# Byte addresses worked out together ahead of the matmuls of a mixture-of-experts tile loop

## The reference, cut to what matters

```python
def _L0_ffn_ref(x, W1, W2, Wr):          # E, DFF, TOPK = 8, 512, 2
    probs = softmax(einsum('btd,ed->bte', x, Wr))
    topk_vals, topk_idx = top_k(probs, 2)
    gate = topk_vals / topk_vals.sum(-1) at topk_idx, 0 elsewhere
    h = silu(einsum('btd,efd->btef', x, W1))
    y = einsum('btef,edf->bted', h, W2)
    return einsum('bte,bted->btd', gate, y)
x = layernorm(x + _L0_ffn_ref(x, W1, W2, Wr))
```

## Time and profile before

| | |
|---|---|
| median of three runs | 1368.81 us |
| profiled execution | 1367.97 us |
| its span, first to last instruction | 1366.2 us |
| TensorE matmul busy | 1071.8 us, 78% |
| VectorE busy | 857.5 us, 63% |
| ScalarE busy | 700.8 us, 51% |
| GpSimd busy | 478.8 us, 35% |
| mean granted TensorE clock | 0.90 of full speed |

### The profile page before, as it was taken

One profiled execution on the slowest core, in us unless ns is written; L12 is line 12 of the kernel. 1 busy time (PEld: TensorE's weight loads), 2 busy tenths in 40 slices (PEclk: granted clock), 3 DMA queues, 4 the chain that ended last, 5 costly groups with the idle time before them and its releaser, 6 DMA issues.

```text
span 1366.2 us, 33527 instructions
## 1 busy us (share of the span) xinstructions
PE 1071.8 (78%) x11050; PEld 875.2 (64%) x11051; DVE 857.5 (63%) x2570; ACT 700.8 (51%) x1284; POOL 478.8 (35%) x588
## 2 busy tenths in 40 slices
PE   3888888884999999999997510079999999999992
PEld 2777777873888888888876300066666666666672
DVE  3788888884788888888886660034445444444451
ACT  3666666663776776767763400044444444444441
POOL 3233333332010010010002427716555655565555
PEclk9999988896999999999997555589999999999996
DMA  6900000000000000000000001121111111111100
GB/s 184 186 17 15 15 15 15 15 9 18 13 11 21 10 10 19 10 18 11 0 1 1 1 16 53 53 57 34 42 37 44 32 36 40 40 35 36 41 17 1
DMA packets 91572, 42.03 MB, mean 31 GB/s; under 512 B 46146, under 2 KB 87372, under 8 KB 91524
## 3 DMA queue, kind: packets, MB, share of 16 engines
q1 hardware_dynamic: 86532, 32.83, 11.2%
q0 software_dynamic: 4992, 8.54, 2.0%
HBM read 20.57 MB, written 16.57 MB: 27 GB/s over the span
## 4 chain that ended last, share of the span: by engine, by line
PE 50%; DVE 20%; issue 12%; ACT 12%; POOL 4%; DMA 0%; DVEq 0%; POOLq 0%; ACTq 0%; SPq 0%
PE bank L439 15%; PE bank L440 12%; PE bank L441 10%; PE bank L541 5%; POOL xd L395 3%; DVE at L912 3%; ACT XTa L745 3%; PE bank L527 3%; ACT qz L745 3%; DVE X L989 3%; DVE mx L896 3%; PE bank L518 2%; DVE st L979 2%; ACT vz_self L754 1%; DVE XTa L888 1%
## 5 line engine op out<-in xcount | busy, mean ns | idle before, releaser
L823 ACT ACTIVATE pr<-bank 128x512 f32<-128x512 f32 x92 | 55.0, 597 | 264.4 <-PE bank L441 262.6
L439 PE MATMUL bank<-XTa,qz 128*128 128x128 f16 x768 | 145.2, 225 | 37.8 <-ACT XTa L745 37.8
L912 DVE TENSOR_TENSOR at<-bank,rc 64x32 f32<-64x32 f32 (+1 forms) x768 | 153.5, 200 | 14.4
L439 PE MATMUL bank<-cth,W 128*128 128x128 f16 x384 | 88.3, 230 | 86.5 <-DMA cth<-xd 85.5
L759 ACT ACTIVATE pr<-bank 128x512 f32<-128x512 f32 x192 | 114.1, 594 | 78.7 <-PE bank L518 77.5
L331 POOL TENSOR_SCALAR ve<-mv 128x4 f32<-128x4 f32 x55 | 12.9, 235 | 396.2 <-DVE mv L983 240.9
L896 DVE TENSOR_REDUCE mx<-bank 128x8 bf16<-128x512 f32 x192 | 132.9, 692 | 26.3 <-PE bank L441 20.7
L441 PE MATMUL bank<-XTa,qz 128*128 128x128 f16 x768 | 145.8, 226 | 0.0
L440 PE MATMUL bank<-XTa,qz 128*128 128x128 f16 x768 | 145.7, 226 | 0.0
L763 ACT ACTIVATE pt<-bank 128x512 f32<-128x512 f32 x192 | 113.2, 590 | 59.5 <-PE bank L527 59.1
L1079 DVE TENSOR_TENSOR ql<-pr,qh 128x512 f16<-128x512 f32 x46 | 49.1, 1068 | 145.5 <-ACT qh L824 143.2
(11 more groups left out here) (209 smaller groups left out, 3516.1 us busy)
## 6 DMA issues: line engine op xcount, KB each, us to landing
xd<-blank SPq DMA_DIRECT2D x1, 6072.0 KB, 35.0
X<-xd SPq DMA_DIRECT2D x23, 264.0 KB, 2.9
X<-x_dram SPq DMA_DIRECT2D x16, 256.0 KB, 2.8
wst<-w_dram SPq DMA_DIRECT2D x16, 256.0 KB, 2.7
cin<-ctx_in_dram SPq DMA_DIRECT2D x16, 256.0 KB, 2.9
out_dram<-X,dest POOLq DMA_INDIRECT x92, 2.3
mraw<-mask_dram SPq DMA_DIRECT2D x32, 32.0 KB, 2.7
xd<-XTa,pos POOLq DMA_INDIRECT x64, 2.3
```

Source lines behind the costliest of these rows:

```text
L439: nc.tensor.matmul(out_, lh, rh, start=start, stop=False, **kw)
L823: nc.scalar.activation(s32[n % 4][:], bank[n % 4][:], ACT.Silu, scale=IWS)
L912: m = nc.vector.tensor_tensor(dst, src, r, ALU.mult)
```

## The change

`up` and `down` call it ahead of their loop over f; in `down` it stands after the two waits. The matmuls, their operands and their order are the same, and so are all other engines' programs.

```diff
@@ -645,6 +645,7 @@
+            W8 = W12[:].bitcast(U8)
             H, Y = bank[0:4], bank[4:8]
             pairs = pe.alloc_register("pairs")
@@ -655,13 +656,19 @@
             def offsets(word, k):
-                return [pe.snap(word // E ** (2 * k + 1 - e) % E * (2 * DFF)) for e in range(2)]
+                return [pe.snap(word // E ** (2 * k + 1 - e) % E * (4 * DFF)) for e in range(2)]
+
+            def weights(at, stationary):
+                v = [W8[:, bass.ds(at + 2 * P * n, 2 * P)].bitcast(F16) for n in range(2 * FC)]
+                for ap in v:
+                    pe.lower_ap(ap, for_matmul_weights=stationary)
+                return [v[2 * f:2 * f + 2] for f in range(FC)]
 
             def up(q, e, base):
                 r = slice(q % 2 * P, q % 2 * P + P)
+                w1 = weights(base[e], True)
                 for f in range(FC):
-                    w = base[e] + f * 2 * P
-                    m = three(H[(2 * q + e) % 4][:, f * P:(f + 1) * P], (W1[:, bass.ds(w, P)], W1[:, bass.ds(w + P, P)]),
+                    m = three(H[(2 * q + e) % 4][:, f * P:(f + 1) * P], w1[f],
                               (xt[q // 2][:, 0, r], xt[q // 2][:, 1, r]), start=f == 0, skip_group_check=True)
                 m.then_inc(f_h, 1)
@@ -670,10 +677,10 @@
                 if e == 0 and not (isinstance(i, int) and i < 4):
                     pe.wait_ge(f_z, i - 3)
+                w2 = weights(base[e] + 4 * E * DFF, False)
                 for f in range(FC):
-                    w = base[e] + f * 2 * P
                     c = slice(f * P, (f + 1) * P)
-                    m = three(Y[q % 4][:, e * P:(e + 1) * P], (sh[n][:, c], sl[n][:, c]), (W2[:, bass.ds(w, P)], W2[:, bass.ds(w + P, P)]),
+                    m = three(Y[q % 4][:, e * P:(e + 1) * P], (sh[n][:, c], sl[n][:, c]), w2[f],
                               start=e == 0 and f == 0, stop=e == 1 and f == FC - 1, skip_group_check=True)
```

## The result

The changed kernel takes 1265.53 us (median of four runs, 1264.09 to 1270.33) against 1368.22 us for the kernel before: a ratio of 0.925, 95% interval 0.922 to 0.929. Forecast were 1248 us and a range of 1232 to 1294: the sign and the bound were right, the size of the gain was 120 us on paper and 103 in fact. The profiled execution is the one of 1264.09 us, with a span of 1262.2.

What follows compares the result with a forecast made beforehand. Register arithmetic ahead of TensorE's matmuls bound the old kernel; POOL's ring would bind next. First give 913.1, 21 rings of 14.25, last give 11.5, tail 21.3, plus 1.8 and 0.8: 1248 us, range 1232 to 1294.

Steps and rivals of the forecast that it cites:

- Bound of the kernel before: Tile loop: register arithmetic ahead of TensorE's matmuls sets the pace, 0.25 us a triple against the array's 0.17.
- The batch's price: B, cost of working out a group's eight addresses together: three instructions, 0.3 us a group.
- The 0.225 us for the loop's other steps: Per group of TensorE's loop: divisions for the next pair, waits and the table load, 0.225 us.
- Rivals 2, 5 and 6: 2: TensorE stays the bound, 1291 us (0.16); 5: batch saves nothing, 1369 (0.03); 6: batch not packed, slower, 1435 (0.05).
- First give: Start of the loop's first give at 913.1 us: 15.9 + 1.6 + 2.0 behind the first matmul at 893.60.
- last turn: Turn without a take, up to the last give: 11.36 us to its scatters' end, 11.5 with the hand-off.
- tail: From the last give's start to the end of the span: 21.3 us.
- The ring: POOL's give and take, then DVE's mixes and moments releasing the next give: 14.25 us a turn, rival 1 (0.56).
- the hand-over: From take's addition (line 401) to the next give: 1.17 addition, 1.26 DVE mixes to aggregates, 0.1 us hand-off.
- the interference: DVE's low parts lengthening POOL's give: 0.17 us each, four seen before, some six expected, + 0.35 us.
- rival 3: Clock row showing 0.5 after each TensorE stop would be its sign; with rival 2 it reaches up to 1294 us.
- TensorE's slack: In the tile loop TensorE's turn is 11.3 us under the 14.25 us ring, keeping 2.9 us idle a turn.

Runs made afterwards that it cites:

- one scatter: Changed kernel with one of give's four indirect scatters left in, three left out with their waits (three quarters of the output not written): 1193.4 us.
- The byte view alone: Changed kernel keeping byte addresses but without the batch, each address worked out where its matmul is: 1344.9 us.
- the additional operations: Two unneeded POOL operations ahead of line 410 in every give: 1289.0 us in the changed kernel, 1372.1 in the kernel before.
- low part from PSUM: Changed kernel with DVE's low-part subtraction reading the PSUM bank instead of the 32-bit silu in SBUF (output changes): 1255.9 us.
- the last two versions: Changed kernel with the addition and two line 410 operations moved to DVE, 1242.4 us; then also take between second and third scatter, 1221.8 us.
- part of POOL's work on DVE: Changed kernel with the addition ahead of the power and two of four line 410 operations moved from POOL to DVE: 1242.4 us.
- the early take: Changed kernel with take (line 401's addition and its copy) put ahead of give's four scatters instead of behind them: 1259.8 us.

## Why the prediction was right, and where it was not

*Bound of the kernel before.* Right. With the queue relieved, the same matmuls run at 0.056 us, and TensorE's work in a turn falls from 19.6 to 10.7 us (one scatter: 12.05 less its wait) with no other change on TensorE. The byte view alone confirms the price per address.

*The batch's price.* B = 0.3 us in three instructions was taken as a cost that adds to the issue of the matmuls. It is two instructions, and it adds nothing that shows except behind a wait (part of the 0.37 us above): the queue runs ahead, so the group is the array's 12 x 0.056 = 0.67 us and not 0.70. The 0.225 us for the loop's other steps does not show either. This term did not reach the time, because the ring lies above it, as the forecast said. Rivals 2, 5 and 6 are out.

*First give, last turn, tail.* 913.1, 11.5 and 21.3 us against 913.00, 11.60 and 21.3. The three terms of the first give (15.9, 1.6 and 2.0 us) were not measured one by one; what is shown is their sum, 19.35.

*The ring.* Its place was right: the additional operations, free before and dear after, show it. Of its terms the hand-over was right: 1.17 + 1.26 + 0.1 = 2.53 us from T to S, measured 2.55. The mis-sized term is the interference. I had 0.17 us for each of four low parts and 0.35 more for six: 1.03 us in all. It is 1.46 (low part from PSUM). The base was low too, 12.55 - 0.68 - 1.17 = 10.70 for the undisturbed S to T, which is 10.85: the four low parts of the kernel before had cost 0.53 us together, 0.13 each, and not 0.68. Together S to T is 12.31 instead of 11.73: 0.58 of the 0.81 us. The step that failed was to scale by a count: eight cost nearly three times what four did. Where the low parts fall changes too, which fits the rows but was not varied by itself: behind the ring's wait DVE has two of them due at once, and issues them right at the start of give. VectorE and then GpSimd in order of time, changed kernel:

```profile
1047.96 0.37 DVE L1106 BATCH_NORM_AGGREGATE mv<-st 128x2 f32<-128x6 f32 x4
1048.24 0.66 DVE L1086 TENSOR_TENSOR ql<-pr,qh 128x512 f16<-128x512 f32 x1
1048.82 0.68 DVE L1086 TENSOR_TENSOR kl<-pr,kh 128x512 f16<-128x512 f32 x1
```

```profile
1048.49 0.50 POOL L331 TENSOR_SCALAR ve<-mv 128x4 f32<-128x4 f32 x1 [1.25 <-DVE mv L1106]
1049.08 1.33 POOL L333 TENSOR_TENSOR rstd<-ve,mhalf 128x4 f32<-128x4 f32 x1
```

The moments end at 1048.33 and release give; the two subtractions, 1048.24 to 1048.90 and 1048.82 to 1049.50, lie over POOL's lines 331 and 333, which take 0.50 and 1.33 us instead of 0.24 and 1.04. In the kernel before a subtraction lies over line 333 as well (1098.93 to 1099.62), and line 333 takes 1.05 us. POOL does not pay the low parts' full length: eight of 0.69 us are 5.5, and 1.46 came through. How close the two lie where they meet the rows show: line 331 ends at 1048.99, right behind the first subtraction (1048.90), and a subtraction that met the take ended with POOL's copy, up to 1.9 us beyond its 0.69, with one scatter and in the last two versions. In the kernel before that was the subtraction of 1.32 us (it ends at 1111.52, POOL's copy at 1111.57). The forecast read this row, and priced only what the subtractions cost POOL. In the changed kernel no subtraction takes over 0.9 us, so the miss of 0.81 us has nothing of this; with one scatter, and with part of POOL's work on DVE, it lengthens the ring.

*Late gives.* 0.20 us a turn ((0.46 + 0.48 + 1.23 + 1.17 + 0.90) / 21), in five turns whose T to S is above 2.55. The forecast had nothing there. With the additional work on POOL, which gives TensorE room, they are gone. In all five DVE starts its last subtraction ahead of the moments 1.1 to 1.9 us behind T, after waiting 3.7 to 4.6 us for ScalarE, which waits for TensorE. They are the part of TensorE's trouble that comes through the ring, its stops and the clock behind them; how much is the one and how much the other is not separated. What was to speak for rival 3, a clock of 0.5 behind a stop, is there (11 times and 37.5 us in the loop, 1.8 us a turn, from none before), but TensorE does not set the turn by it: in 16 of the 21 turns the ring does. With one scatter, where TensorE waits 1.1 to 1.6 us a turn for DVE, the clock is 1.00. With the additional operations TensorE goes up to 6.6 us from one matmul to the next and the clock falls 13 times, 81.9 us, yet the turn there is exactly S to T plus 2.56: the loss falls into idle time.

*What was said of TensorE's slack.* "TensorE keeps 2.9 us of idle time a turn" did not hold. With 10.7 us of work it should have had over 4; the stops (43.7 us in 21 turns, 2.1 each) and the low clock took most of that. So the kernel sat with two bounds within 0.5 us of one another, and moving one of them (the early take, the low part from PSUM) brought 6 and 10 us instead of 26 and 22. That the stops make the second bound is argued from the late subtractions in those two runs; no run takes the stops away and nothing else. The prediction could not show this: the kernel before has no such stop.

## What to carry to other kernels

When an engine's queue is the bound and not the engine, work out addresses in one batch and in the unit that needs no further step (88 and 24 us here, each by itself); then compute the next ring through the other engines before believing the full gain, with the time from each release to the next start as a term of its own. Interference between two engines should not be scaled by a count alone (four low parts cost POOL 0.53 us a turn here, eight 1.46): look at which operations will lie side by side once the waits have moved, and price both sides, what each engine costs the other. An operation that takes three times its usual length, as the subtraction with one scatter does (2.12 us instead of 0.69), can be a link of the ring though no wait shows there. And when a bound is removed and the gain stays out, look inside the groups of the engine behind it, not only at its waits.

## What the runs showed of the hardware

TensorE stopped in the middle of groups of matmuls with nothing to wait for, mostly 0.3 to 0.8 us from one matmul to the next, within 1.55 us behind the issue of an indirect scatter of GpSimd and never between the first of a give and the second (211 stops in four runs), and only where TensorE's instructions ran at the array's pace (0.056 us a matmul): none at 0.22 or 0.25 us a triple (the byte view alone, and the kernel before). No run with one scatter a turn, or with no more than two in a row, has any; neither has one with four in a row and more arithmetic ahead of them (16.23 us a turn). What makes them is open; the loading of instructions does not (54 of the changed kernel's 63 lie between 937 and 1208 us, where no packet of instructions moves). The loads of the next rows and columns fall into the same stretch (issued at 1011.38 and 1012.65, with the scatters at 1012.06 to 1014.62), and the phase between the two lists, which every one of these runs shifts, was not varied by itself.

A VectorE subtraction with two inputs in SBUF that met GpSimd's addition and copy ended with the copy: 2.12 to 2.57 us instead of 0.69 in the turns with one scatter, 1.32 in the row of the kernel before, each 0.04 us ahead of the copy's end. The other way round, eight of them cost GpSimd 1.46 us a turn in the changed kernel, and with one of the inputs in PSUM nothing of the kind shows: give's start to the take is 10.75 to 10.89 us in every turn.

Addresses of matmul operands cost TensorE's queue about 0.10 us each when they stand singly (0.11 to 0.13 us between loads less 0.015). Eight together ahead of a group, in two register instructions, cost nothing that shows (groups mostly follow one another at 0.056 us), except behind a wait, where 0.37 us pass from the wait's end to the first load.
